# Four-layer graph network on one core: a tile-wise start of layer 2, work shared out at its end, a node cell with its biases on TensorE, and points in bf16

## The reference

```
x = norm(x + relu(D (adj + I) D (x W0) + b0))                        # layer 1
x = norm(x + relu(softmax(leaky(f1 + f2.T) where adj > 0) @ (x W1))) # layer 2
x = norm(x + [pos, neg] @ Wn + (adj @ x) @ We + (bn + be) * diag)    # layer 3
edge = gru(adj0 @ x, x);  node = gru(mean of 3 attention heads, x)   # layer 4
x = norm(x + diag * edge + diag * node)
```

## Time and profile before

| | |
|---|---|
| median of 3 runs | 1569.28 us (1567.17 to 1570.38) |
| the profiled execution | 1568.71 us, its span 1567.0 us |
| TensorE busy | 1378.0 us, 88% |
| VectorE busy | 939.5 us, 60% |
| ScalarE busy | 537.1 us, 34% |
| GpSimd busy | 171.2 us, 11% |
| HBM | 203 GB/s over the span |

### The profile page before, as it was taken

One profiled execution on the slowest core, in us unless ns is written; L12 is line 12 of the kernel. 1 busy time (PEld: TensorE's weight loads), 2 busy tenths in 40 slices (PEclk: granted clock), 3 DMA queues, 4 the chain that ended last, 5 costly groups with the idle time before them and its releaser, 6 DMA issues.

```text
span 1567.0 us, 12683 instructions
## 1 busy us (share of the span) xinstructions
PE 1378.0 (88%) x4557; PEld 725.9 (46%) x4557; DVE 939.5 (60%) x1388; ACT 537.1 (34%) x419; POOL 171.2 (11%) x196
## 2 busy tenths in 40 slices
PE   3787885579994999998999999799999999999982
PEld 1333333434443444445555455545545454544561
DVE  4888886458876000002025363598778987898587
ACT  3343431447743000000110001355555556455321
POOL 0000000420000000001000000133111321125100
PEclk9999897689997999999899999999999999999996
DMA  9999990000003666665566427588786878688101
GB/s 364 405 405 401 406 381 10 2 1 0 0 0 103 195 193 195 194 183 173 175 207 203 146 81 245 197 302 306 271 299 225 321 284 294 229 319 312 66 1 44
DMA packets 99919, 318.82 MB, mean 203 GB/s; under 512 B 11009, under 2 KB 26240, under 8 KB 86272
## 3 DMA queue, kind: packets, MB, share of 16 engines
q1 hardware_dynamic: 99840, 317.83, 57.9%
HBM read 314.38 MB, written 3.41 MB: 203 GB/s over the span
## 4 chain that ended last, share of the span: by engine, by line
PE 75%; DMA 11%; DVE 8%; issue 2%; POOL 2%; ACT 1%; SPq 1%; DVEq 0%
PE ps L1082 27%; DMA ring<-in_adjB 11%; PE ps L842 10%; PE ps L925 9%; PE ps L889 9%; PE ps L883 5%; PE ps L781 4%; PE ps L987 2%; POOL y L488 2%; PE ps L1003 1%; DVE x L1197 1%; PE ps L906 1%; PE ps L1064 1%; PE ps L907 1%; PE ps L866 1%
## 5 line engine op out<-in xcount | busy, mean ns | idle before, releaser
L1082 PE MATMUL ps<-arena,x 128*128 128x512 f32 (+1 forms) x1092 | 443.3, 564 | 10.4 <-DVE arena L1589 8.8
L1082 PEld LDWEIGHTS ps<-arena,x 128*128 128x128 f32 x1092 | 205.7, 191 | 239.7 <-issue 226.5
L702 ACT ACTIVATE arena<-arena,bench 128x3328 f32<-128x3328 bf16 x78 | 239.6, 3073 | 201.0 <-PE ps L1082 197.3
L781 PE MATMUL ps<-ring,bench 128*128 128x512 f32 (+1 forms) x364 | 174.9, 627 | 43.3 <-DMA ring<-in_adjB 43.3
L1589 DVE TENSOR_TENSOR arena<-arena,ring 128x3328 f32<-128x3328 f32 x52 | 189.3, 3640 | 38.9 <-ACT arena L702 38.9
L889 PE MATMUL ps<-ring,x 128*128 128x512 f32 (+1 forms) x364 | 175.7, 564 | 0.0
L925 PE MATMUL ps<-ring,x 128*128 128x512 f32 (+1 forms) x364 | 157.1, 585 | 3.7 <-DVE x L1197 3.7
L1322 DVE SCALAR_TENSOR_TENSOR bench<-b,cols,ps 128x128 f32<-128x128 f32 x26 | 7.3, 343 | 208.1 <-PE ps L866 208.1
L781 PEld LDWEIGHTS ps<-ring,bench 128*128 128x128 f32 x364 | 72.2, 209 | 125.4 <-issue 83.2
L883 PE MATMUL ps<-arena,shared 128*128 128x512 fp8e4 (+1 forms) x364 | 103.5, 366 | 16.1 <-DVE shared L1317 16.1
L1589 DVE TENSOR_TENSOR arena<-arena 128x3328 f32<-128x3328 f32 x26 | 94.3, 3627 | 19.1 <-ACT arena L702 19.1
(11 more groups left out here) (254 smaller groups left out, 1506.2 us busy)
## 6 DMA issues: line engine op xcount, KB each, us to landing
ring<-in_adjB SPq DMA_DIRECT2D x468, 256.0 KB, 3.6
ring<-in_adjR SPq DMA_DIRECT2D x52, 1664.0 KB, 7.7
arena<-in_adjR SPq DMA_DIRECT2D x26, 1664.0 KB, 7.7
shared<-in_adj SPq DMA_DIRECT2D x7, 1664.0 KB, 14.5
es<-in_adj SPq DMA_DIRECT2D x7, 1664.0 KB, 14.2
xT<-in_adj SPq DMA_DIRECT2D x6, 1664.0 KB, 14.6
ring<-in_adjB SPq DMA_DIRECT2D x78, 128.0 KB, 2.5
y<-in_adj SPq DMA_DIRECT2D x6, 1664.0 KB, 14.4
```

What stands on the lines that cost most here:

```text
L702: A_(E[n % 3], below[n % 3], ACT.Exp, bias=tt_[:, t * HEADS + k:t * HEADS + k + 1], scale=-WIN).then_inc(e_exp, 1)
L781: mm(ps[:, b, 0:w], lhsT=scaled[:, t % 4], rhs=ring[:, n % CHUNKS, 0:w], start=(t == 0), stop=(t == TILES - 1)).then_inc(ring_free, 1)
L1082: last = mm(ps[:, b, 0:w], lhsT=x[:, t], rhs=E[n % 3][:, o_:o_ + w], start=(t == 0), stop=(t == TILES - 1))
```

## The change

- **End of layer 1:** `finish0` is written out for all groups, its buffer is `hb4` with room for two groups, and a group's statistics come after the next group's first step.
- **Start of layer 2:** ScalarE takes 5 score blocks (`RP_ACT`), each as soon as it is there, VectorE the last two (`scores_rest`). Tile 0 goes in two parts (`PARTS`, 2048 and 1280 columns). GpSimd writes the one column first, and TensorE waits per tile. VectorE's four small steps for `xsb` move behind tile 4 (`faint_row`).
- **End of layer 2:** banks 1, 3 and 5 are copied out by VectorE, the others by ScalarE; GpSimd adds `x`.
- **Norm 1:** `split_x` runs inside `norm(1)`, after each second tile.
- **Points:** `MN` and the identity they are multiplied with (`ident16`) are bf16.
- **Node cell:** the biases are split into three bf16 rows during the load pass (`split_bias`, at tile 4) and added by a TensorE product over 3 rows; columns of the gates are rolled on the host so that each tile has one bias product and two of 384 columns. ScalarE reads PSUM for the tanh, GpSimd subtracts `x - n`, three work spaces replace two. The last head uses bank 7 twice (`LAST_BANKS`); `es_done` is gone and waits on `zh_out` per block take its place. The edge cell has three products a tile in place of four, with as many columns.

```diff
-MN = sb("MN", [P, TILES, HEADS])
+MN = sb("MN", [P, TILES, HEADS], BF16)
+ident16 = gb[:, 1].rearrange("p a f -> p (a f)")[:, 3 * F:3 * F + P // 2].bitcast(BF16)
...
-two_spaces = [Cells(ring_flat[:, 16 * F * par:16 * F * (par + 1)]) for par in range(2)]
+three_spaces = [Cells(ring_flat[:, 16 * F * n:16 * F * (n + 1)]) for n in range(3)]
...
+bias_parts = node_bias[:, 0:2 * F].bitcast(BF16)
+ones16 = node_bias[:, 2 * F:2 * F + P // 2].bitcast(BF16)
+part_, taken = (piece(bench, 2 * GW + n * GW, GW)[0:3].bitcast(BF16) for n in range(2))
...
+RP_ACT, FIRST = 5, 4
+PARTS = [(0, FIRST * MAX_WIDTH), (FIRST * MAX_WIDTH, NP)]
...
+LAST_BANKS = (7, 0, 1, 2, 3, 4, 7)
+def NG(par):
+    return ps[:, 2 * par:2 * par + 2, :]
+def NU(par):
+    return ps[:, 5 + par, 0:GW]
...
+    g_.tensor_copy(y[:, :, F - 1:F], fade[:, :, None]).then_inc(xp_done, 1)
     for t in range(TILES):
-        g_.tensor_scalar(y[:, t], x[:, t], fade[:, t:t + 1], None, ALU.mult).then_inc(xp_done, 1)
-    pool.wait_ge(xp_done, TILES)
-    g_.tensor_copy(y[:, :, F - 1:F], fade[:, :, None]).then_inc(xp_done, 1)
+        g_.tensor_scalar(y[:, t, 0:F - 1], x[:, t, 0:F - 1], fade[:, t:t + 1], None, ALU.mult).then_inc(xp_done, 1)
+    def layer2(general):
+        if general:
+            return
+        for k in range(GROUPS):
+            pool.wait_ge(z_out, 2 + GROUPS + k + 1)
+            g_.tensor_tensor(y[:, 2 * k:2 * k + 2], hb4[:, 2 * (k % 2):2 * (k % 2) + 2], x[:, 2 * k:2 * k + 2],
+                             ALU.add).then_inc(y_done, 1)
+    either(pool, layer2, 1)
...
+    for g in range(GROUPS):
+        w = three_spaces[g % 3]
+        pool.wait_ge(n_done, GROUPS + g + 1)
+        g_.tensor_tensor(w.hm, x[:, 2 * g:2 * g + 2], w.n, ALU.subtract).then_inc(hm_done, 1)
...
-    for b, (o_, w) in enumerate(BLOCKS):
-        act.wait_ge(f1_done, NB)
+    for b, (o_, w) in enumerate(BLOCKS[:RP_ACT]):
+        act.wait_ge(f1_done, b + 1)
         A_(rp[:, o_:o_ + w], ps[:, b, 0:w], ACT.Relu, bias=spans[:, 0:1]).then_inc(rp_done, 1)
...
+            elif t == 0:
+                for n, (lo, hi) in enumerate(PARTS):
+                    act.wait_ge(low1_part, n + 1)
+                    A_(EL[0][:, lo:hi], EL[0][:, lo:hi], ACT.Exp, scale=ALPHA - 1).then_inc(exp1_part, 1)
...
         for b, (o_, w) in enumerate(BLOCKS):
-            if b == 0:
-                act.wait_ge(used1, TILES)
-                act.wait_ge(small, XSB_READY)
-            A_(UT[:, o_:o_ + w], ps[:, b, 0:w], ACT.Identity, bias=xsb).then_inc(ut1, 1)
-            if b >= 2:
-                relu_pair(2 * b - 4)
-                relu_pair(2 * b - 3)
-        for k in range(2 * NB - 4, GROUPS):
+            if b % 2 == 0:
+                A_(UT[:, o_:o_ + w], ps[:, b, 0:w], ACT.Identity, bias=xsb).then_inc(ut1, 1)
+                if b >= 4:
+                    relu_pair(b // 2 - 2)
+        for k in range(2, GROUPS):
             relu_pair(k)
...
+    for g in range(GROUPS):
         act.wait_ge(u7_done, g + 1)
         ge(act, g3_done, GROUPS + g - 1)
-        A_(ub[:, g % 2, 0:GW], UA(g % 2), ACT.Copy, scale=1.0 / HEADS).then_inc(u7_out, 1)
+        A_(ub[:, g % 2, 0:GW], NU(g % 2), ACT.Copy, scale=1.0 / HEADS).then_inc(u7_out, 1)
         if g >= 2:
-            gru_cand(GROUPS + g - 2, two_spaces[g % 2])
+            node_cand(g - 2)
         if g >= 1:
-            gru_tanh(GROUPS + g - 1, two_spaces[1 - g % 2])
-    for g in range(GROUPS):
...
-        pe.wait_ge(xp_done, TILES + 1)
         for t in range(TILES):
-            pe.wait_ge(q1, t + 1)
+            pe.wait_ge(xp_done, t + 2)
+            if t:
+                pe.wait_ge(q1, t)
             for b, (o_, w) in enumerate(BLOCKS):
+                if t == 0 and b in (0, FIRST):
+                    pe.wait_ge(q1_part, 1 if b == 0 else 2)
                 op = mm(ps[:, b, 0:w], lhsT=y[:, t], rhs=EL[t % 4][:, o_:o_ + w], start=(t == 0), stop=(t == TILES - 1))
             op.then_inc(used1, 1)
         for k in range(GROUPS):
-            pe.wait_ge(ut1, max(k // 2 + 1, k if k < NB else 0))
+            last = max(k // 2, k - 1 if k < NB else 0)
+            pe.wait_ge(ut1, last // 2 + 1)
+            ge(pe, ut1_odd, (last + 1) // 2)
...
-            mm(gt[:, G3:4 * F], lhsT=ht, rhs=gru[:, 2 * e + 1, 2 * F:], start=True, stop=True)
-            mm(gt[:, 2 * F:G3], lhsT=ut, rhs=gru[:, 2 * e, 2 * F:], start=True, stop=True)
-            mm(gt[:, 0:2 * F], lhsT=ut, rhs=gru[:, 2 * e, 0:2 * F], start=True, stop=False)
-            last = mm(gt[:, 0:2 * F], lhsT=ht, rhs=gru[:, 2 * e + 1, 0:2 * F], start=False, stop=True)
+            mm(gt[:, G3:4 * F], lhsT=ut, rhs=gru[:, 0, 2 * F:], start=True, stop=True)
+            mm(gt[:, 0:G3], lhsT=ht, rhs=gru[:, 1], start=True, stop=False)
+            last = mm(gt[:, F:G3], lhsT=ut, rhs=gru[:, 0, 0:2 * F], start=False, stop=True)
...
-            last = mm(ps[:, bank, tt * P:(tt + 1) * P], lhsT=MN[:, t, k:k + 1].to_broadcast([P, P]), rhs=ident[:],
+            last = mm(ps[:, bank, tt * P:(tt + 1) * P], lhsT=MN[:, t, k:k + 1].to_broadcast([P, P]), rhs=ident16,
...
-    pe.wait_ge(es_done, 1)
     def node_gates(g):
         pe.wait_ge(u7_out, g + 1)
-        gate_products(GROUPS + g, 1, ub[:, g % 2], 0, g * GW)
+        if g < 2:
+            pe.wait_ge(zh_out, (HEADS - 1) * NB + 3 + 2 * g)
+        else:
+            pe.wait_ge(cand_done, GROUPS + g - 1)
+        for tt in range(2):
+            gt = NG(g % 2)[:, tt]
+            ut = ub[:, g % 2, tt * P:(tt + 1) * P]
+            ht = xT[:, g * GW + tt * P:g * GW + (tt + 1) * P]
+            mm(gt[:, 0:4 * F], lhsT=ones16, rhs=bias_parts, start=True, stop=False)
+            mm(gt[:, F:4 * F], lhsT=ut, rhs=gru[:, 2], start=False, stop=False)
+            last = mm(gt[:, 0:G3], lhsT=ht, rhs=gru[:, 3], start=False, stop=True)
+        last.then_inc(g3_done, 1)
...
+        pe.wait_ge(zh_out, (HEADS - 1) * NB + g // 2 + 1)
...
-            last = nc.tensor.transpose(ps[:, g % 2, tt * P:(tt + 1) * P], es[:, g * 2 + tt], ident[:])
+            last = nc.tensor.transpose(NU(g % 2)[:, tt * P:(tt + 1) * P], es[:, g * 2 + tt], ident[:])
...
+    def split_bias():
+        for n in range(3):
+            step(v.tensor_copy(part_, node_bias))
+            if n < 2:
+                step(v.tensor_tensor(node_bias, node_bias, part_, ALU.subtract))
+            mask = ident[0:3, n:n + 1]
+            if n == 0:
+                step(v.tensor_scalar(taken, part_, mask, None, ALU.mult))
+            else:
+                step(v.scalar_tensor_tensor(taken if n == 1 else bias_parts, part_, mask, taken, ALU.mult, ALU.add))
+        step(v.tensor_copy(ones16, ones[0:3, :]))
+        step(v.tensor_copy(ident16, ident[:]))
...
+        if t == 4:
+            split_bias()
...
-    def finish0(g, par, n):
+            if layer == 1 and t % 2:
+                split_x(t // 2)
...
+    def finish0(g):
         ve.wait_ge(z_done, 2 + g + 1)
         for tt in range(2):
-            op = v.scalar_tensor_tensor(hb[:, tt], Z0(par)[:, tt], column(D, g * 2 + tt), b0[:], ALU.mult, ALU.add)
+            op = v.scalar_tensor_tensor(hb4[:, g % 2 * 2 + tt], Z0(g % 2)[:, tt], D[:, 2 * g + tt:2 * g + tt + 1], b0[:], ALU.mult, ALU.add)
         op.then_inc(z_out, 1)
+        if g:
+            statistics0(g - 1)
         ve.wait_ge(z_out, 2 + g + 1)
-        v.scalar_tensor_tensor(y[:, bass.ds(g * 2, 2)], hb[:], 0.0, x[:, bass.ds(g * 2, 2)], ALU.max,
-                               ALU.add).then_inc(y_done, 1)
-        statistics(0, g)
-    groups(ve, finish0)
+        v.scalar_tensor_tensor(y[:, 2 * g:2 * g + 2], hb4[:, g % 2 * 2:g % 2 * 2 + 2], 0.0, x[:, 2 * g:2 * g + 2],
+                               ALU.max, ALU.add).then_inc(y_done, 1)
+    for g in range(GROUPS):
+        finish0(g)
+    statistics0(GROUPS - 1)
...
-    ve.wait_ge(xT_done, NB)
...
+    def faint_row():
...
+    def scores_rest():
+        for b, (o_, w) in enumerate(BLOCKS):
+            if b >= RP_ACT:
+                ve.wait_ge(f1_done, b + 1)
+                v.tensor_scalar(rp[:, o_:o_ + w], ps[:, b, 0:w], spans[:, 0:1], 0.0, ALU.add, ALU.max).then_inc(rp_rest, 1)
...
+        def cut_part(n):
+            lo, hi = PARTS[n]
+            v.tensor_scalar(EL[0][:, lo:hi], rp[:, lo:hi], gap[:, 0:1], None, ALU.min).then_inc(low1_part, 1)
+        def weigh_part(n):
+            lo, hi = PARTS[n]
+            ve.wait_ge(exp1_part, n + 1)
+            v.tensor_tensor(EL[0][:, lo:hi], EL[0][:, lo:hi], pos8[:, 0, lo:hi], ALU.mult).then_inc(q1_part, 1)
...
-        ve.wait_ge(rp_done, NB)
-        cut_scores(0)
+        ve.wait_ge(rp_done, FIRST)
+        cut_part(0)
+        scores_rest()
+        ve.wait_ge(rp_done, RP_ACT)
+        ve.wait_ge(rp_rest, NB - RP_ACT)
+        cut_part(1)
         cut_scores(1)
-        for t in range(TILES):
+        weigh_part(0)
+        weigh_part(1)
+        for t in range(1, TILES):
             if t + 2 < TILES:
                 cut_scores(t + 2)
             weigh(t)
```

(46 more changed lines are left out.)

139 lines of the change are left out of this document (84 added, 55 removed).

## The result

The changed kernel takes **1514.01 us** (median of 4 runs, 1512.74 to 1517.6) against 1568.22 for the kernel before on the same chip (1566.36 to 1570.38): a ratio of 0.9657, 95% interval 0.9646 to 0.9669. The profiled execution took 1513.72 us with a span of 1512.0.

A forecast was written before the change was run, and what follows sets the result against it. TensorE, holding 75% of the span, was taken as the bound, with holes to close. Gains of 5.8 + 16.0 + 2.4 + 9.5 + 11.1 + 15.5 = 60.3 us from 1568.7, plus 0.6, gave 1509.0 us; range 1498 to 1527.

The forecast's parts named there:

- Load pass: VectorE's ten small steps at tile 4, some 4 us, hidden while DMA is late and so costed at nothing.
- End of layer 1: Written-out groups of layer 1 take 1.45 us each instead of 1.95, between floor 1.25 and 1.61; gain 5.8 us.
- Start of layer 2: TensorE's first layer 2 product comes 16.8 us earlier, less small losses at later tiles; gain 16.0 us.
- End of layer 2: GpSimd's addition, taken as 0.80 us, sets the pace of 13 groups; stage 13.8 us for 16.2, gain 2.4.
- Norm 1: From first scaling of x to layer 3's first product 1.5 us instead of 11.04; gain 9.5 us.
- Points: 78 point products in the heads' part of TensorE's chain, 0.08 us each in bf16 for 0.223; gain 11.1 us.
- Node cell: TensorE sets the pace at 3.3 us a group for 4.34, each bias product costing one 0.215 us pass; gain 15.5.
- B: Node cell keeps a wait through GpSimd and extra hand-overs: groups 4.0 us apart, not 3.3, 1518 us; chance 0.16.
- A: Layer 2 starts early and runs dry: 25 tiles lose 0.3 us each, 7.5 us in all, 1516; chance 0.14.
- C: VectorE shuts GpSimd out in layer 2, TensorE at GpSimd's pace: at 9 us a tile 1582 us; chance 0.03.
- D: Point products do not shrink as forecast because their weight loads show: 0.15 us each, 1514.5 us; chance 0.07.

## Why the prediction was right, and where not

- **Load pass**, costed at nothing: right. The stage did not grow, so the ten small steps were hidden. Its gain of 0.9 us says nothing: the first step of layer 1 came between 243.6 and 246.0 us in the runs.
- **End of layer 1**, 5.8: it gave 8.9. The mechanism holds, the size was off: I took 1.45 us a group between the floor 1.25 and the row's 1.61, and VectorE reached the floor at 1.24. The statistics fill the wait wholly.
- **Start of layer 2**, 16.8 and -0.8: it gave 15.1 and -1.4. The branch took 4.49 us and not 3.47, a difference that alone explains 1.0 of the 1.7; it was no wait for ScalarE, whose five blocks were done 1.5 us before VectorE's first cut. Undoing the wait alone costs 15.3.
- **End of layer 2**, 2.4: it gave 3.3. GpSimd's addition was taken as 0.80, and is 0.72, paced at 0.76 a group. The Trainium skill's GPSIMD Engine Reference, from whose section 3.1 the estimate of 0.73 was made, hit it, and so did the 12.9 us of its sum for the stage up to the last statistics (462.8 - 449.9); its advice in section 4.1, to keep elementwise work on VectorE, holds for the instruction (0.72 for 0.41) but undoing the step lengthened the stage by 1.9 us.
- **Norm 1**, 9.5: it gave 9.6, and 1.45 us from scaling to product for the 1.5 predicted.
- **Points**, 11.1: over layers 3, 4 and the heads it gave 9.2, undone alone 12.6. I took 0.08 a product; it is 0.055. The Trainium skill, TensorE: Matmul & The Clock Gate, Part 1, with its 56 ns agrees with the trace. In the heads alone the two comparisons agree: 472.7 us before the change and with f32 points, 464.8 in the changed kernel, 7.9 us. They part ahead of the heads, from layer 3's first product to the first lowering: 1.3 us gained against the kernel before, 4.2 against f32 points. That stretch takes 498.7 to 503.0 us in profiles with the same code there, so the difference is not resolved.
- **Node cell**, 15.5: it gave 9.4, and this is the step that failed. "One pass is 0.215, twice a group" priced the pass and left out that a product of 3 rows between products of 128 has its weight load, and the load after it, uncovered: 0.51 us each. 13 groups x 2 x (0.51 - 0.215) = 7.7 us, and over 128 rows the stretch from the last head copy to the last statistics is 59.42 - 51.77 = 7.65 us shorter. Then groups are 3.23 us apart, where the prediction worked out 3.27. All else in the term held: TensorE set the pace, and from the last head product on (56.0 us in all) start and tail took 56.0 - 13 x 3.83 = 6.2 us against 6.8. The term's own numbers, 65.5 - 49.7, make 15.8 and not 15.5.

Of the rivals, **B** named the right place and nearly the right pace (4.0 against 3.83 us), with the wrong cause: no hand-over is waited for, as the runs without the bias and with the subtraction moved show. **A** has 1.4 us for 26 tiles and not 7.5. **C** shows itself at 1.86 us a tile, far from TensorE's 5.75; the single row of 5.79 in the earlier trace rows was no measure of the mean. **D** is out. The sum came out within 5 us partly by luck: what layer 1, the load pass and the end of layer 2 gave beyond their terms (4.9 us) made good most of what the node cell failed to give (6.1). A sum that comes out near does not show that each term did.

The range's lower end is not what its text says. The bounds' gains beyond the forecast are 2.6, 2.0, 1.3, 0.5, 1.9 and 2.5 us, 10.8 in all: 1498 is the forecast with the whole of them, and half of them would give 1503.6.

## What to carry to other kernels

A small product that is put between large ones is not priced by its pass alone: look whether the load ahead of it, and the one after it, still start under the product before. Here, filling its contraction with zeros up to its neighbours' 128 rows cost nothing and won 7.3 us; where rows can't be filled, put such products together. And when a step is moved to a slower engine, compare the queues' totals per group and not the two instructions: the addition became 0.3 us slower and the stage 1.9 us shorter.

## What the runs showed of the hardware

- A bf16 weight load of 3 or 64 rows behind an f32 product of 128 rows starts only when that product is through, and so does the f32 load of 128 rows behind it. A bf16 load of 128 rows in the same place runs under the product ahead, and so does one of 3 rows behind a product of 3 rows. Bias product to the f32 product behind it: 0.31, 0.32 and 0.215 us for 3, 64 and 128 rows.
- From norm 0 to GpSimd's first row of `y` the same code takes 21.2, 22.8 or 24.5 us, and once 23.3. TensorE's granted clock differs. In the run with the subtraction on VectorE (a stretch of 21.2), stages as in the earlier trace rows:

```profile
274.00:276.00 2.00, 2.00 (x14) 2.00 (x14) 0.00 (x0) 0.00 (x0) 0.00 (x0) 0.62 0.00 0
...
278.00:285.00 7.00, 7.00 (x15) 2.76 (x16) 1.85 (x11) 0.68 (x2) 0.40 (x2) 0.76 0.00 0
```

  In the run with the early weighing (24.5):

```profile
272.00:274.00 2.00, 2.00 (x13) 2.00 (x12) 0.00 (x0) 1.09 (x1) 0.00 (x0) 0.58 0.00 0
...
278.00:283.00 5.00, 5.00 (x15) 3.46 (x16) 0.73 (x5) 0.00 (x0) 0.00 (x0) 0.50 0.00 0
```

  Both have 1.00 of the full clock just before the first row shown, and both fall there to 0.50, the lower level of 1.2 GHz, though TensorE has not stopped: it is doing the 52 products of two columns of the score columns (L798 before the change), one behind the other. The first run falls some 2 us later and is back at 1.00 from 282 us on, so that its stage up to 285 averages 0.76; the second still has 0.50 up to 285. The 52 products take 7.43 us in the first and 9.67 in the second. A fall and a rise that come sooner or later are worth 3.3 us here: as much as several of the terms, so single profiles are compared stage by stage, where the clock is the same.
- Reading the flag and branching cost VectorE 3.47 to 4.77 us, with nothing named that it waits for.
